# One semaphore for both summands of the update of q

## The reference

```python
def _derivative(q, p, drive, coupling, bias):
    i_couple = jnp.tanh(q) @ coupling.T
    dq = q - q ** 3 / 3.0 - p + drive + i_couple + bias
    dp = EPSILON * (q + ALPHA - BETA * p)
```

## Time and profile before

| | |
|---|---|
| median of three runs | 743.61 us (742.80 to 743.67) |
| profiled execution, its own time | 745.0 us |
| its span, first to last instruction | 743.1 us |
| mean granted TensorE clock | 0.995 |
| PE busy | 679.2 us, 91% |
| DVE busy | 671.2 us, 90% |
| ACT busy | 431.0 us, 58% |
| POOL busy | 174.6 us, 23% |

### The profile page before, as it was taken

The page is one execution under the profiler, slowest core; times in us unless marked ns, Lnnn a source line. Parts: engine busy times, 40 slices in busy tenths (PEclk is TensorE's granted clock), DMA queues, the critical chain, the costliest instruction groups (busy, mean ns, idle before and its releaser), DMA issues.

```text
span 743.1 us, 33477 instructions
## 1 busy us (share of the span) xinstructions
PE 679.2 (91%) x12101; PEld 601.7 (81%) x12101; DVE 671.2 (90%) x4624; ACT 431.0 (58%) x2310; POOL 174.6 (23%) x372
## 2 busy tenths in 40 slices
PE   2437999999999999999999999999999999999998
PEld 1326888888888888888888888888888989888888
DVE  5899999999999999999999999999999899999972
ACT  3865646556565655656565565656556565654643
POOL 0001221312222231222223122221312213132233
PEclk9999999999999999999999999999999999999999
DMA  8600000000000000000000000000000000000000
GB/s 319 189 2 2 3 3 11 4 9 4 10 3 3 11 3 10 4 10 4 3 11 3 11 2 11 2 4 10 4 10 4 10 4 2 11 4 10 4 9 9
DMA packets 8630, 13.64 MB, mean 18 GB/s; under 512 B 1520, under 2 KB 7984, under 8 KB 8208
## 3 DMA queue, kind: packets, MB, share of 16 engines
q1 hardware_dynamic: 8464, 11.50, 4.5%
HBM read 9.40 MB, written 2.10 MB: 15 GB/s over the span
## 4 chain that ended last, share of the span: by engine, by line
PE 62%; DVE 22%; issue 7%; ACT 3%; POOL 3%; DMA 2%; SPq 0%; DVEq 0%; POOLq 0%; ACTq 0%
PE up_ps L507 18%; PE down_ps L521 14%; PE coup_ps L456 12%; PE coup_ps L449 11%; PE warm_ps L537 5%; DVE th_lo L685 2%; POOL hidden L839 2%; PE route_ps L488 2%; DMA wf<-in_w_up 2%; DVE q L720 2%; DVE p_part L623 2%; DVE q_raw L720 1%; DVE w L618 1%; DVE p_sum L643 1%; DVE force L707 1%
## 5 line engine op out<-in xcount | busy, mean ns | idle before, releaser
L507 PE MATMUL up_ps<-q_hi,w 128*128 128x128 f16 x2176 | 226.5, 220 | 0.7 <-POOL q_lo L809 0.7
L449 PE MATMUL coup_ps<-th_hi,c 128*128 128x16 f16 x4096 | 183.2, 171 | 30.1 <-ACT th_hi L348 27.8
L449 PEld LDWEIGHTS coup_ps<-th_hi,c 128*128 128x128 f16 x4096 | 148.0, 97 | 71.3 <-ACT th_hi L348 48.0
L348 ACT ACTIVATE th_hi<-q 128x32 f16<-128x32 f32 x384 | 88.0, 229 | 189.0 <-DVE q L720 187.3
L507 PE MATMUL up_ps<-q_lo,w 128*128 128x128 f16 x1088 | 197.2, 220 | 0.0
L839 POOL TENSOR_TENSOR hidden<-hidden,comb_s 128x128 f32<-128x128 f32 x272 | 124.5, 459 | 295.4 <-PE coup_ps L456 274.4
L507 PEld LDWEIGHTS up_ps<-q_hi,w 128*128 128x128 f16 x2176 | 175.0, 98 | 0.8 <-POOL q_lo L809 0.8
L521 PE MATMUL down_ps<-hidden,wd 128*128 128x128 f32 x1088 | 157.8, 285 | 0.0
L456 PE MATMUL coup_ps<-th_lo,c 128*128 128x16 f16 x2048 | 132.2, 173 | 24.3 <-DVE th_lo L685 17.1
L521 PEld LDWEIGHTS down_ps<-hidden,wd 128*128 128x128 f32 x1088 | 133.3, 191 | 0.0
L456 PEld LDWEIGHTS coup_ps<-th_lo,c 128*128 128x128 f16 x2048 | 85.8, 97 | 58.5 <-DVE th_lo L685 32.5
(11 more groups left out here) (87 smaller groups left out, 910.0 us busy)
## 6 DMA issues: line engine op xcount, KB each, us to landing
wf<-in_w_up SPq DMA_DIRECT2D x1, 4224.0 KB, 13.5
wd<-in_w_down SPq DMA_DIRECT2D x1, 2048.0 KB, 22.4
out<-out_s SPq DMA_DIRECT2D x16, 128.0 KB, 2.1
xs<-in_x SPq DMA_DIRECT2D x1, 1920.0 KB, 19.0
sel<-in_spread SPq DMA_DIRECT2D x1, 408.0 KB, 18.8
cf<-in_coupling SPq DMA_DIRECT2D x1, 256.0 KB, 2.4
xs<-in_x SPq DMA_DIRECT2D x1, 128.0 KB, 2.2
ident<-in_identity SPq DMA_DIRECT2D x1, 64.0 KB, 2.3
```

What stands on the lines that cost most here:

```text
L348: nc.scalar.activation(th_hi[:], q[:], ACT.Tanh).then_inc(hi_ready, 1)
L449: nc.tensor.matmul(coup_ps[:, m * B:(m + 1) * B], c16[:, part, k, m * P:(m + 1) * P], th_hi[:, k, :], start=part == m == k == 0, stop=Fals ...
L507: last = nc.tensor.matmul(up_ps[j % 4][:, h * TOK:(h + 1) * TOK], w16[:, part, k, h, j * P:(j + 1) * P], q[:, k, :], start=n == 0, stop=n ...
```

## The change

The semaphores `coupled` and `forced` are replaced by one, `summands`. Force and the last matmul of th_lo both raise it by one, and the update of q waits once, for 2(n + 1). POOL, which waited for `coupled`, waits for the same value of `summands`. No arithmetic changes, and the order of instructions on each engine stays.

```diff
--- before.py
+++ after.py
@@ -209,9 +209,8 @@
         tanh_ready = sem("tanh_ready")
         squared = sem("squared")
         lo_ready = sem("lo_ready")
-        coupled = sem("coupled")
+        summands = sem("summands")
         cubed = sem("cubed")
-        forced = sem("forced")
         rested = sem("rested")
         p_summed = sem("p_summed")
         p_clipped = sem("p_clipped")
@@ -455,7 +454,7 @@
                     for k in range(KC):
                         last = nc.tensor.matmul(coup_ps[:, m * B:(m + 1) * B], c16[:, 0, k, m * P:(m + 1) * P],
                                                 th_lo[:, k, :], start=False, stop=True, skip_group_check=True)
-                last.then_inc(coupled, 1)
+                last.then_inc(summands, 1)
 
             def ffn(f, st):
                 first_block = isinstance(f, int) and f == 0
@@ -704,7 +703,7 @@
                                             ).then_inc(p_clipped, 1)
 
                 dve.wait_ge(cubed, n + 1)
-                nc.vector.tensor_tensor(force[:], rest[k][:], cubic[:], ALU.subtract).then_inc(forced, 1)
+                nc.vector.tensor_tensor(force[:], rest[k][:], cubic[:], ALU.subtract).then_inc(summands, 1)
                 if k == 0:
 
                     dve.wait_ge(based, t + 1)
@@ -715,8 +714,7 @@
                     dve.wait_ge(p_clipped, t + 1)
                     parts_of_p(0)
 
-                dve.wait_ge(forced, n + 1)
-                dve.wait_ge(coupled, n + 1)
+                dve.wait_ge(summands, 2 * (n + 1))
                 nc.vector.scalar_tensor_tensor(
                     q_raw[:] if k == 3 else q_in[k + 1][:], coup_ps[:, 0:CB].rearrange("p (m b) -> p m b", m=KC),
                     c_un[:, (0, 0, 2, 3)[k]:(0, 0, 2, 3)[k] + 1], force[:], ALU.mult, ALU.add
@@ -843,7 +841,7 @@
                 for st in range(STAGES):
                     if f is not None:
 
-                        pool.wait_ge(coupled, b * STAGES + st + 1)
+                        pool.wait_ge(summands, 2 * (b * STAGES + st + 1))
                         ffn(f, st)
 
             blocks(one_block)
```

## The result

The changed kernel takes 730.32 us (median of 4 runs, 729.92 to 730.59), against 743.64 for the kernel before (4 runs, 742.80 to 743.74): ratio 0.9823, 95% interval 0.9806 to 0.9840. It is 13.3 us faster. The forecast was 724.1, with a range of 719 to 732. The profiled execution of the changed kernel took 729.92 with a span of 728.1: 15.1 and 15.0 less than that of before.

What follows compares the result with a forecast made beforehand. It took a ring through DVE, ACT and PE as the bound: 23.6 us gained at q, less 4.1 swallowed by PE, is 19.5; 745.0 less that is 725.5, and 1.4 lower for the median gives 724.1, range 719 to 732.

Steps and rivals of the forecast that it cites:

- The ring: Per stage: q (DVE), th_hi (ACT), th and th_lo, low-half matmuls (PE), q again; claimed to bound most of 512 stages.
- The release (0.12 and 0.035): At q: PE's release through the separate wait costs 0.12 us, any other 0.035; 0.085 is the detour.
- the forecast's 16.3: Idle before q, stages k = 0 to 2: 25.3 us less the 9.0 that stays, a gain of 16.3.
- Rival 1: At q: only the separate wait's instruction goes, not the rest of the detour; gain 9 us, time 734; chance 0.08.
- rival 2: At q: the separate wait costs nothing and PE's release takes 0.12 anyway; no change, 743.6 us; chance 0.04.
- rival 3: At q: two increments on one semaphore hold each other up; slower, 753 or at the far bound 773 us; chance 0.04.
- k = 3: 128 stages with p_part between force and q: 4.7 us idle before q_raw goes, plus 2.6; gain 7.3 us.
- PE's absorption: Stages after 18, 22, 26, 29 and 30, 75 in all: PE's down matmuls swallow q's gain, 4.1 us lost.
- Cost 0: POOL at each stage's head now waits for force too, 0.03 to 0.13 us later; claimed to cost nothing.
- The bound of 16 us: POOL's later start without cover: some 8 k = 0 stages with weighing x 15 x 0.13, 16 us at most.
- k = 1 and 2: 256 stages where q waits 0.12 after PE: idle before q falls to 9.0 us, gain 16.3 before PE's share.
- the k = 0 without a hold: 128 stages k = 0, where q already starts 0.04 after late force: gain 0, in a few up to 0.085.

Runs made afterwards that it cites:

- swap_waits: The kernel before, with its two waits of q in the other order (coupled first, then forced): 755.55 us, ratio 1.0157.
- met_wait: The changed kernel, with a separate wait put back before q, for a semaphore met long before (cubed of the same stage): 729.86 us, ratio 0.9810.
- The two narrowed kernels: The kernel before and the changed kernel, each with POOL's weighing cut to one column of 128 in stages k = 3: 736.98 and 719.03 us.
- clip_mixed: The changed kernel, with the clip of q ahead of rest in every step, and ahead of p_part in stages 16, 20, 24, 28 from block 1: 723.58 us.
- best: pool_by_clip, with the clip of q also put ahead of rest in stages 8, 12, 16, 20 and 24: 714.02 us, ratio 0.9601.
- pool_by_clip: The changed kernel, with POOL in stages k = 3 waiting for the clip of p instead of both summands: 720.75 us, ratio 0.9695.

## Why the prediction was right, and where it was off

The sign and the mechanism of the gain were right; its size on the path was put 4.5 us too large. The 730.3 measured lie just above the 719 to 730 that the prediction made from its own terms; the range as given holds them only by the 2 us added for the rivals. That margin was not meant for the loss that came, so this part is luck.

- The ring as the bound: right. What q no longer waits the stages no longer last: shorter are 24 of the 32 stages of a block by 0.01 to 0.12 (medians over the blocks, from q to q).
- The release (0.12 and 0.035): right, in size and in kind. Idle before q went from 25.3 to 9.3 us, the forecast's 16.3 to 0.3 us; swap_waits and met_wait show the mechanism. Rival 1 and rival 2 fall by these two; rival 3 by the timeline above, where both increments come within 0.03 us and q starts 0.03 behind the later. In the medians over blocks 1 to 15, q starts 0.035 behind force in 23 of the 24 stages k = 0, 1 and 2 of a block, and 0.038 behind PE's end where PE is the later (19, 23, 27, 30, 31).
- k = 3: q_raw does start sooner after PE, but its idle time fell only from 4.7 to 3.4, for where PE is late DVE still waits for PE itself (stages 19 and 23 hold 3.9 of it before and 3.2 after). The row's idle time was not all detour, as I had it.
- PE's absorption: right where it was put. Stage 18 to 19 kept its 1.48 us between low halves. In the medians the low halves of stages 23, 27 and 30 kept their distance from the ones before, too, within 0.001 us; that of 31 came 0.013 sooner.
- POOL: the step that failed. I wrote "Cost 0" and looked only at who waits for POOL. What mattered was whom POOL keeps from running. The p_part behind q_raw is held while POOL runs, POOL starts with PE's end where PE is late (in stage 15 force is now the later, and POOL starts by it), and so the clip, the square and, as k = 0 is bound by force, the next q stay where they were. The whole gain of q_raw was swallowed in the stages 16, 20, 24 and 28 of a block, which got longer by 0.06 to 0.08 us each. Summed from q to q over the blocks, these 60 stages lost 4.5 us, and 19.5 - 4.5 = 15.0, as between the spans. The two narrowed kernels, where the hold is gone, are 17.95 us apart. The kernel before held p_part already (0.33 long); the earlier trace rows end at q_raw, one instruction short of it. The bound of 16 us beside "Cost 0" is a slip as well: a block has 4 stages k = 0 with weighing (16, 20, 24, 28), not 8.
- The rest: stage 14 gave nothing either, since the rest at its head (line 674) is held in the same way (0.28 us before, 0.36 after); stage 4 gave 1.0 us, for a reason left open. That 15.0 comes out to the tenth is partly chance. By kind of stage, from q to q: k = 1 and 2 gave 13.0 us where the forecast, less PE's share, had 15.5; k = 3 gave 4.7 for 4.0; the k = 0 without a hold gave 1.8 for 0. These differences nearly cancel. The last 1.7 us between 15.0 and 13.3 are that the profiled execution before was 1.4 above its median, and the one after 0.4 below.

## What to carry to other kernels

Where two waits stand in front of an instruction on the ring, find out which one became an instruction of its own; it should be the one met first, or there should be one semaphore. Before a gain on a ring is added up, follow the side engine whose start hangs on the ring's old event: its instructions hold others, and what they hold doesn't move. A pacing wait, which guards no data, is worth a try at another event.

## What the hardware showed beside this

- DVE instructions with two inputs in SBUF that began in the first 0.3 us of POOL's weighing were held: p_part up to 0.41 for 0.21. So was the clip, which has one input: 0.25 in clip_mixed for 0.17 in best. Instructions that began 0.38 or more behind POOL's start were not held (p_sum 0.18 to 0.19 in the changed kernel). q and hidden, which read PSUM, kept their 0.25 and 0.34. The hold goes both ways: POOL's instruction took 0.50 to 0.51 in pool_by_clip, where a p_part had started first, and 0.45 to 0.46 in the other stages of that kernel. The Trainium skill, "Advanced Engine Details and Errata", section "Miscellaneous Facts", has that POOL shares a read and a write interface with DVE and conflicts with its instructions that have two SBUF inputs or run in a two-port mode; the traces agree for two inputs, and that the clip runs in such a mode no run here shows.
- Timeline of clip_mixed, the held clip:

```profile
...
383.97 0.45 POOL L849 TENSOR_TENSOR hidden<-hidden,comb_s 128x128 f32<-128x128 f32 x1 [0.99 <-PE coup_ps L455]
...
384.21 0.25 DVE L666 TENSOR_SCALAR q_trace<-q_raw 128x32 f32<-128x32 f32 x1
```

- Stage 4 of a block, behind the router's exponent on POOL (1.64 us), takes 1.41, 1.56 or 1.71 us in the kernel before, from block to block (1.64 once), and 1.44 in nearly all blocks of the changed one. Why was not settled; 1.0 of the 15.0 us between the two spans lies there.
